# First attention layer: the probabilities of a step turned by one DMA transpose of 512 KB in place of two of 256 KB

## The reference

```python
x = x + _L0_xattn_ref(_layernorm(x), ctx, Wq, bq, Wkv, bkv, Wo, bo)   # 32 heads of 128, 8 kv heads
x = x + _L0_ffn_ref(_layernorm(x), ...)                               # relu^2 512-1024-512 and a routed latent part
x = x + _L1_xattn_ref(_layernorm(x), ctx, ...)                        # 32 heads of 16, 8 kv heads
x = x + _L1_ffn_ref(_layernorm(x), ...)                               # 8 experts, the mean of the top two
```

```python
scores = jnp.einsum('blkgd,bmkd->bkglm', q, k) * scale   # 64 queries by 64 keys for each head and sequence
attn = jax.nn.softmax(scores, axis=-1)
o = jnp.einsum('bkglm,bmkd->blkgd', attn, v).reshape(B, L, NHEAD * HDIM)
return o @ Wo + bo
```

## Time and profile before

| | |
|---|---|
| median of 3 runs | 1761.13 us (1760.33 to 1764.64) |
| the profiled execution | 1759.08 us, span 1757.3 us |
| PE busy | 1684.8 us, 96% of the span, 12480 matmuls |
| DVE busy | 1200.8 us, 68% |
| ACT busy | 709.4 us, 40% |
| GpSimd busy | 524.6 us, 30% |
| DMA transposes of the first layer (L1341) | 64, issued between 57.2 and 985.4 us |

### The profile page before, as it was taken

How to read it: one execution, slowest core, us unless ns; L and a number is a source line. 1 busy time by engine, 2 the same in 40 slices (tenths; PEclk the granted TensorE clock), 3 DMA queues, 4 the chain that set the end, 5 groups by cost and what they waited for, 6 DMA issues and landing times. The chain is left out here.

```text
span 1757.3 us, 31909 instructions
## 1 busy us (share of the span) xinstructions
PE 1684.8 (96%) x12480; PEld 887.0 (50%) x12480; DVE 1200.8 (68%) x2269; ACT 709.4 (40%) x1290; POOL 524.6 (30%) x401
## 2 busy tenths in 40 slices
PE   5879999999999999999999999998999999999998
PEld 2445555555555555555555444444444545455443
DVE  6786666665656656656566667777878888888873
ACT  5543333333333333333333433233544555545442
POOL 4143560701605307117500110010023333332334
PEclk9899999999999999999999999999999999999999
DMA  7031150411512404215421130112544544545440
GB/s 270 13 92 42 49 180 13 144 49 25 168 25 62 131 14 127 66 25 181 133 74 25 45 118 1 25 25 52 194 98 80 93 76 91 91 83 92 74 83 19
DMA packets 235373, 142.57 MB, mean 81 GB/s; under 512 B 219232, under 2 KB 219488, under 8 KB 227296
## 3 DMA queue, kind: packets, MB, share of 16 engines
q1 hardware_dynamic: 167648, 123.82, 26.3%
q10 hardware_dynamic: 67584, 16.79, 5.4%
HBM read 65.60 MB, written 20.97 MB: 49 GB/s over the span
## 5 line engine op out<-in xcount | busy, mean ns | idle before, releaser
L813 PE MATMUL bank<-R 128*128 128x512 f16 (+1 forms) x7152 | 1295.6, 341 | 28.7 <-DVE X L1800 11.6
L813 PEld LDWEIGHTS bank<-R 128*128 128x128 f16 x7152 | 585.1, 98 | 678.0 <-issue 34.9
L1712 DVE SCALAR_TENSOR_TENSOR R<-bank,biases,R 128x512 f16<-128x512 f32 x288 | 204.6, 746 | 221.1 <-ACT R L1295 178.2
L668 POOL TENSOR_TENSOR R<-R 128x512 f32<-128x512 f32 x112 | 144.8, 1293 | 321.9 <-ACT R L1504 319.6
L1295 ACT ACTIVATE R<-bank,biases 128x512 f16<-128x512 f32 x128 | 87.7, 686 | 271.6 <-PE bank L813 267.3
L524 POOL TENSOR_SCALAR R<-R 128x2048 f32<-128x2048 f32 (+1 forms) x21 | 34.8, 1656 | 385.4 <-PE bank L813 351.8
L1504 ACT ACTIVATE R<-R,msk 128x512 f32<-128x512 f32 x128 | 90.1, 718 | 118.2 <-DVE R L2081 118.1
L1800 DVE SCALAR_TENSOR_TENSOR X<-bank,X 128x512 f32<-128x512 f32 x128 | 86.7, 683 | 33.5 <-PE bank L813 33.4
L1724 DVE SCALAR_TENSOR_TENSOR R<-bank,R 64x512 f16<-64x512 f32 x64 | 44.0, 688 | 94.7 <-ACT R L1303 94.2
L2081 DVE SCALAR_TENSOR_TENSOR R<-bank,R 128x512 f32<-128x512 f32 x128 | 85.4, 679 | 29.5 <-PE bank L813 28.8
L1303 ACT ACTIVATE R<-bank 64x512 f16<-64x512 f32 x128 | 75.6, 591 | 50.7 <-PE bank L813 49.6
(11 more groups left out here) (161 smaller groups left out, 1630.4 us busy)
## 6 DMA issues: line engine op xcount, KB each, us to landing
R<-in_wB SPq DMA_DIRECT2D x16, 1024.0 KB, 5.1
R<-in_wX SPq DMA_DIRECT2D x16, 1024.0 KB, 4.8
w_split<-AW SPq DMA_DIRECT2D x16, 1024.0 KB, 4.8
R<-w_split SPq DMA_DIRECT2D x12, 1024.0 KB, 7.4
R<-in_ctxT SPq DMA_DIRECT2D x4, 1024.0 KB, 9.9
X<-in_x SPq DMA_DIRECT2D x4, 1024.0 KB, 13.7
out<-X SPq DMA_DIRECT2D x16, 256.0 KB, 2.0
R<-in_wB SPq DMA_DIRECT2D x7, 512.0 KB, 5.6
```

Source lines behind the costliest of these rows:

```text
L668: g.tensor_tensor(acc, acc, tmp[:, e % 2, :], ALU.add).then_inc(e_acc, 1)
L813: last = pe.matmul(dst, a(sa), b(sb_), start=(k == 0), stop=(k == m - 1))
L1712: v.scalar_tensor_tensor(out=dst, in0=src, scalar=bias, in1=hi, op0=ALU.add, op1=ALU.subtract).then_inc(done, 1)
```

## The change

ACT issues one transpose of all 2048 columns of `PPb` in place of two of 1024 columns. It waits for both `plo` and for all four products of the step before. One semaphore `t_in` takes the place of two, and all four `b_pv` of a step and both `phi` of the next one wait for it. Its place in ACT's order is that of the former pair.

```diff
-        t_in = [sem("t_in0"), sem("t_in1")]
+        t_in = sem("t_in")
...
             def b_pv(s, jb):
-                pe.wait_ge(t_in[jb // 2], (s + 1) * 16)
+                pe.wait_ge(t_in, (s + 1) * 16)
...
                 def phi(hf):
                     act.wait_ge(s_prob, s * 2 + hf + 1)
-                    w(act, t_in[hf], s * 16)
+                    w(act, t_in, s * 16)
...
-                def turn(hf):
-
-                    act.wait_ge(s_plo, s * 2 + hf + 1)
-                    w(act, o_mm, s * 4 - 2 + 2 * hf)
-                    act.dma_start_transpose(PTb[:, hf * 1024:(hf + 1) * 1024].rearrange("p (k n) -> p k n", n=P),
-                                            PPb[:, 8 * hf:8 * hf + 8].rearrange("p k s m -> p (k s m)")).then_inc(t_in[hf], 16)
+                def turn():
+
+                    act.wait_ge(s_plo, s * 2 + 2)
+                    w(act, o_mm, s * 4)
+                    act.dma_start_transpose(PTb.rearrange("p (k n) -> p k n", n=P),
+                                            PPb.rearrange("p k s m -> p (k s m)")).then_inc(t_in, 16)
...
-                    turn(0)
-                    turn(1)
+                    turn()
```

## The result

| kernel | runs | median (us) | lowest to highest |
|---|---|---|---|
| before | 9 | 1762.59 | 1759.61 to 1764.64 |
| changed | 9 | 1768.32 | 1763.61 to 1773.73 |

The ratio is 1.0044, with a 95% interval of 1.0031 to 1.0057: 7.7 us slower (5.5 to 10.0), where 4.0 were forecast. The two medians of the table are 5.7 us apart, which lies inside that interval; the ratio isn't their quotient. On the median of before that stood with the prediction, 1761.13, the forecast was 1765.1, and its range ended at 1768.5, so that the measured 1768.32 lies just inside it.

What follows compares the result with a forecast made beforehand. The prediction took PE as the bound, busy 805.22 of 809 us in steps 3 to 30. Its terms, 0.2 + 0.9 + 1.4 + 1.5 = 4.0 us, on a median of 1761.13 gave 1765.1 us, range 1761.5 to 1768.5.

Steps and rivals of the forecast that it cites:

- Price of the transpose on its own: Each 128 by 2048 transpose: 4.2 us from issue to landing, 1.94 us of ACT's queue.
- Middle steps: Steps 3 to 30 but for 26: the transpose lands before PE wants it, so 27 steps cost nothing.
- Steps 1 and 2: First product with V: PE waits for the later landing, 0.2 us in step 1 and 0.9 us in step 2.
- Step 26: The transpose starts behind SP's two 1 MB transfers and lands late; PE waits 1.2 to 2.2 us, 1.4 taken.
- the term for ACT's queue: Middle steps: queue held 1.94 us in place of 2 x 1.27, the saving worth nothing; no cost entered in step 26.
- Step 31: Last step, no projection to hide the transpose: product 1.75 us later, o_part(0) 1.25 us late; 1.5 us taken.
- rival (a): Slower by over 0.3%: longer wait in step 31 lowers PE's clock, also step 2; 7.3 us, 1768.4; chance 0.27.
- the high bound: Landing in 4.9 us, with the worst case of 2.2 us in step 26: 7.1 us in all, 1768.2.
- The sum: Steps 1, 2, 26 and 31 together: 0.2 + 0.9 + 1.4 + 1.5 = 4.0 us slower.

Runs made afterwards that it cites:

- e2: The changed kernel with the two small transposes back in steps 26 and 31 only; median 1761.11 us, ratio to before 1.0000.
- e4: The changed kernel, but in step 26 SP waits until the transpose has landed before its 1 MB store and load; median 1763.30 us, ratio to before 1.0020.
- e7: The changed kernel, but in step 26 SP's 1 MB load, not its store, waits until the transpose has landed; 1763.76 us in one run.
- e3: The kernel before with its two small transposes, both held until the large one could start; median 1768.08 us, ratio to before 1.0044.
- e5: The changed kernel, but in step 26 ACT does proj(1) before it issues the transpose; median 1764.60 us, ratio to before 1.0021.
- e0_after_again: The changed kernel measured again without any edit; median 1768.59 us, ratio to before 1.0043.

## Why the prediction was wrong

- **Price of the transpose on its own: right.** 4.2 us at least and 4.3 at the median against 4.2 forecast, 1.83 us of queue against 1.94. The 3.2 us for 512 KB from the fit in the Trainium skill ("DMA: Bandwidth & Descriptors", section "Anatomy of one DMA") was too little, as the rows had it; the page gives that fit for DMAs issued by GpSimd, and these come from ACT and SP.
- **Middle steps: right but for 26.** From step 3 to 25 the lead of before doesn't grow (2.9 to 2.7 us), and behind 26 to step 30 neither (8.8).
- **Steps 1 and 2: the waits are right.** PE waits 0.85 us for the transpose in step 2 against 0.9 forecast, and in step 1 for 0.17 us in e2 against 0.2. What they add to the time, 0.3 and 0.7 us in this pair of profiles, is within what executions differ by.
- **Step 26: this is the step that failed.** The sum had 1.4 us, worked out as a late landing: "landing at 849.5 to 850.5, and PE waits 1.2 to 2.2 us where it waited for nothing". The measured price is 5.0 to 6.1 us, and it isn't the landing. The transpose landed at 852.4, which is 849.7 in the times of the kernel before (2.7 us earlier, the lead in step 25), within the forecast; but PE came to it 4.7 us after that. What failed is the term for ACT's queue: the prediction took it from L468's median of 1.94 us, wrote for the middle steps that "what is saved there is worth nothing", and put nothing for it in step 26. It had the row that speaks against it: the two issues of step 26 took 1.92 and 2.83 us where 1.27 is usual. And the timeline of before at step 26 shows no cover left:

```profile
838.78 4.84 ACTq L1341 DMA_TRANSPOSE AW<-AW  x2
...
843.75 0.69 ACT L1295 ACTIVATE R<-bank,biases 128x512 f16<-128x512 f32 x1 [5.19 <-PE bank L813]
```

  The queue came free at 843.62, and ACT wrote the high half of projection 1 at 843.75, as soon as PE had it. An issue that starts only at 840.31, with the end of the second L1786, has 3.4 us until then; one of 7.33 us is 3.9 us too long, and PE waited 3.47. What the runs showed in its place is that the issue is held longer the more SP has put ahead of it there (e4, e7, changed: 1.86, 4.67, 7.33 us for 0, 1 and 2 MB), that the late start and not the size brings it there (e3), and that PE then waits for the bank that ACT and DVE can't empty (e5). The late landing is a real price only where the queue is out of the way, 1.15 us of wait in e5.
- **Step 31: the mechanism right, the size off.** 1.5 us forecast, 2.3 measured. The wait is 1.8 us longer, as forecast; ACT's `o_part(0)` followed it nearly in full (999.18 against 988.51: 10.7 us, of which 8.8 are older), and the clock after the longer pause added to it (8 matmuls at L859 in 1.89 us in place of 1.05, at a granted clock of 0.51 from 998.0 to 1001.4 where the kernel before had 0.83 from 987.4 to 990.2).
- **The clock of rival (a)** was a part of what happened, behind step 26: 12 matmuls in 5.30 or 4.10 us where 2.75 is usual, 2.6 and 1.3 us. The pause that brought it there was not the one named, a longer wait in step 31. So it is luck that the 1768.4 of (a) meets the measured median, and that this median lies inside the range: the largest term of the sum was neither in (a) nor in the high bound, which held at most 2.2 us for step 26.
- **The sum.** 0.3 + 0.7 + 5.0 to 6.1 + 2.3 is 8.3 to 9.4 us; less the 0.2 given back that is within the interval of the ratio, 5.5 to 10.0. With step 26 at its measured price and the rest as forecast the sum would have been 7.6 to 8.7.
- **Still open**: why the queue is held longer behind SP's transfers, and why two small transposes behind the same 2 MB are issued in 2.11 and 5.07 us. The runs show that it is, and not whether a limit on what the DMA engines hold or something else in the issue is what makes ACT wait. SP's own issues of 1 MB, with nothing of ACT's ahead, took 0.35 and 0.43 us. It is also open whether a store and a load count alike: e7 has the store ahead, and no run has the load alone.

## What to carry to other kernels

A DMA issued from a computing engine's queue costs that engine its issue time, and the issue time is not a constant (1.33 to 7.33 us for the 32 transposes here): look at the longest issue of the line and at what another queue put ahead of it, not at the median alone. When two transfers are merged, the first loses its early start; what was ahead of a collision may now fall behind it. Ask of every instruction that stands behind such an issue how long its reader can wait, before asking when the data lands.

## What was not expected of the hardware

- The issue of one DMA transpose on ACT's queue took 1.86 us with nothing of SP's under way (e4), 4.67 us with 1 MB of SP's just issued (e7), and 7.33 us with 2 MB; two of half the size took 7.28 us together (e3). The other 31 issues of the changed kernel took 1.33 to 2.99 us.
- The Trainium skill ("DMA: Bandwidth & Descriptors", section "Issuing engines are not separate DMA queues") says that the time a sequencer takes to initiate a DMA is usually small relative to the DMA itself. Here it was 7.33 us of the 9.4 us to landing, and 1.83 of 4.3 us at the median.
- A wait of PE of 3.47 us in an otherwise full stretch was followed by a granted clock of 0.57 over 8 us (0.79 in e0_after_again, behind 3.50 us), and the 12 matmuls behind the wait took 2.6 us longer than usual (1.3 in e0).
